# A multi-expert Flamingo block: ScalarE takes the exponential while it evacuates the transposed scores, in both attentions

## The reference, cut to what matters

```python
x = x + tanh(gx[0]) * attention16(layernorm(x), ctx, ctx)   # 16 heads of 8 channels, softmax(q k / sqrt(8)) v
x = x + tanh(gf[0]) * experts_top2(layernorm(x))            # per token: the 2 best of 8 experts
x = x + tanh(gx[1]) * attention1(layernorm(x), ctx, ctx)    # 1 head of 128 channels, causal
x = x + tanh(gf[1]) * experts_choice(layernorm(x))          # per sequence: each of 8 experts picks 17 tokens
```

## Time and profile before

| | |
|---|---|
| time, median of 3 runs | 1260.38 us (1259.9 to 1260.52) |
| profiled execution: span from first to last instruction | 1044.2 us |
| median less that span | 216.2 us |
| TensorE busy | 927.7 us (89%) |
| VectorE busy | 624.5 us (60%) |
| ScalarE busy | 581.2 us (56%) |
| GpSimd busy | 679.4 us (65%) |
| ScalarE, exponentials of layer 0 (L1669) | 32, first 25.7, last 286.1 us |
| ScalarE, exponentials of layer 1 (L1802) | 16, first 618.3, last 708.6 us |

### The profile page before, as it was taken

One profiled execution on the slowest core, in us unless ns is written; L12 is line 12 of the kernel. 1 busy time (PEld: TensorE's weight loads), 2 busy tenths in 40 slices (PEclk: granted clock), 3 DMA queues, 4 the chain that ended last, 5 costly groups with the idle time before them and its releaser, 6 DMA issues.

```text
span 1044.2 us, 25012 instructions
## 1 busy us (share of the span) xinstructions
PE 927.7 (89%) x8892; PEld 777.6 (74%) x8892; DVE 624.5 (60%) x1600; ACT 581.2 (56%) x1274; POOL 679.4 (65%) x905
## 2 busy tenths in 40 slices
PE   5999988788748999999999989887998999999992
PEld 3777776566647989999999977775776767778881
DVE  5899999988964563244625759784735424533320
ACT  2888876687525446544644667554555455444540
POOL 6565556578747777377427777621686758878785
PEclk9999998899868999999999999998999999999997
DMA  9355432122145656676566663123164554574444
GB/s 367 117 177 183 153 123 100 38 67 68 52 157 161 209 176 205 201 213 188 163 193 187 195 236 103 43 71 90 17 114 49 91 68 50 81 105 54 51 54 45
DMA packets 130811, 130.87 MB, mean 125 GB/s; under 512 B 33410, under 2 KB 103426, under 8 KB 129794
## 3 DMA queue, kind: packets, MB, share of 16 engines
q1 hardware_dynamic: 100466, 91.82, 27.8%
q0 software_dynamic: 28928, 29.91, 17.5%
q10 hardware_dynamic: 1296, 7.54, 1.8%
HBM read 54.01 MB, written 49.62 MB: 99 GB/s over the span
## 4 chain that ended last, share of the span: by engine, by line
PE 57%; DVE 13%; ACT 9%; DMA 7%; issue 7%; POOL 6%; ACTq 0%; SPq 0%; POOLq 0%; DVEq 0%
PE psum L844 10%; PE psum L854 10%; PE psum L1022 9%; PE psum L1012 8%; PE psum L656 3%; ACT w_sb L1669 3%; PE psum L976 2%; POOL work L1970 2%; DVE mx L1156 2%; DVE w_sb L1162 2%; ACT work L1676 1%; PE psum L834 1%; DMA out_x<-ln_sb,dest 1%; PE psum L683 1%; DMA odd<-ln_sb,dest 1%
## 5 line engine op out<-in xcount | busy, mean ns | idle before, releaser
L1763 ACT ACTIVATE hid_sb<-psum,work 128x128 f32<-128x128 f32 (+1 forms) x424 | 145.6, 412 | 138.9 <-PE psum L844 136.6
L1970 POOL DMA_INDIRECT work<-yg,place x128 | 122.7, 959 | 73.6 <-issue 48.2
L844 PE MATMUL psum<-work 128*128 128x128 f32 (+1 forms) x848 | 150.1, 320 | 2.6 <-issue 2.3
L854 PE MATMUL psum<-w_sb,hid_sb 128*128 x1192 | 150.2, 275 | 0.0
L854 PEld LDWEIGHTS psum<-w_sb,hid_sb 128*128 128x128 f32 x1192 | 144.8, 192 | 2.1
L1012 PE MATMUL psum<-work,w_sb 128*128 128x272 f32 (+2 forms) x512 | 131.0, 397 | 5.1 <-ACT ctx_sb L1872 3.1
L2044 POOL DMA_INDIRECT out_x<-ln_sb,dest x68 | 106.2, 1562 | 45.0 <-DVE ln_sb L1586 24.8
L844 PEld LDWEIGHTS psum<-work 128*128 128x128 f32 x848 | 124.4, 192 | 11.3 <-issue 4.2
L1872 ACT ACTIVATE ctx_sb<-psum,w_sb 128x272 f32<-128x272 f32 (+2 forms) x256 | 115.8, 488 | 26.3 <-PE psum L1012 22.5
L1022 PE MATMUL psum<-ctx_sb,w_sb 128*128 128x272 f32 (+2 forms) x512 | 128.1, 392 | 0.0
L2044 POOL DMA_INDIRECT odd<-ln_sb,dest x68 | 105.5, 1552 | 32.3 <-issue 16.1
(11 more groups left out here) (241 smaller groups left out, 1762.3 us busy)
## 6 DMA issues: line engine op xcount, KB each, us to landing
work<-w_sb SPq DMA_DIRECT2D x76, 322.0 KB
work<-xg SPq DMA_DIRECT2D x73, 128.0 KB
yg<-yg_sb SPq DMA_DIRECT2D x73, 128.0 KB
xg<-yg_sb SPq DMA_DIRECT2D x24, 384.0 KB, 4.1
ctx_sb<-tok SPq DMA_DIRECT2D x8, 1088.0 KB, 6.4
ctxn<-sums_sb SPq DMA_DIRECT2D x64, 64.0 KB, 2.0
out_x<-x_sb SPq DMA_DIRECT2D x16, 256.0 KB
odd<-yg_sb SPq DMA_DIRECT2D x10, 384.0 KB, 2.9
```

The costliest lines, as they stand in the source:

```text
L844: e.matmul(banks[UP_BANKS[c]][:, 0:cols], w1g(b)[:, c * P:c * P + P], xgT_sb[:, u % 2, at:at + cols], start=True, stop=True).then_inc(s_up, 1)
L854: ins = e.matmul(banks[DOWN_BANKS[b % 2]][:, n * D:n * D + D], hid0[:, b % 2, c, n * P:n * P + P], w2_sb[:, bass.ds(number, 1), c, :].rear ...
L1763: e.activation(hid0[:, b % 2, c, 0:cols], banks[UP_BANKS[c]][:, 0:cols], ACT.Gelu, bias=w1g(b)[:, HID + c:HID + c + 1]).then_inc(s_hg, 1)
L1970: e.indirect_dma_start(dst[:, k, :], None, yg_dram[h], at).then_inc(s_get[i], 16)
```

## The change: what it does

The pass of ScalarE over the row layout is gone in both attentions (L1669 and L1802), with the semaphores that it raised. TensorE transposes the shifted scores themselves, once VectorE has written them. ScalarE's evacuation of the transposed chunks, a copy before, is an activation with the exponential and the scale.

```diff
             def turn_p(p, chunks):
                 i = p % 2
-                w.wait_ge(s_exp, p + 1)
+                w.wait_ge(s_sub, p + 1)
...
             def turn1(g):
-                w.wait_ge(s_e1, g + 1)
+                w.wait_ge(s_sub1, g + 1)
...
-            def exponentials(p):
-                flat = pr[:, p % 2, :, :, :, :].rearrange("p j u h k -> p (j u h k)")
-                w.wait_ge(s_sub, p + 1)
-                e.activation(flat, flat, ACT.Exp, scale=SCALE0).then_inc(s_exp, 1)
-
-            def copy_p(p, chunks):
+            def exponentials(p, chunks):
                 for n in chunks:
                     u, half = n // 2, n % 2
                     w.wait_ge(s_pt, 4 * p + n + 1)
                     w.wait_ge(s_av, p - 1)
-                    e.copy(pT[:, p % 2, u, 4 * half:4 * half + 4, :], banks[B_T[half]]).then_inc(s_pT, 1)
+                    dst = pT[:, p % 2, u, 4 * half:4 * half + 4, :].rearrange("p r q -> p (r q)")
+                    e.activation(dst, banks[B_T[half]], ACT.Exp, scale=SCALE0).then_inc(s_pT, 1)
...
-                if p < NP:
-                    exponentials(p)
...
             def exponentials1(g):
-                flat = p1[:, g % 2, :, :].rearrange("p t k -> p (t k)")
-                w.wait_ge(s_sub1, g + 1)
-                e.activation(flat, flat, ACT.Exp, scale=SCALE1).then_inc(s_e1, 1)
-
-            def copy_p1(g):
                 w.wait_ge(s_pt1, g + 1)
                 w.wait_ge(s_o1, g - 1)
-                e.copy(pT1[:, g % 2, :], banks[3]).then_inc(s_pT1, 1)
+                e.activation(pT1[:, g % 2, :], banks[3], ACT.Exp, scale=SCALE1).then_inc(s_pT1, 1)
...
-                if 0 <= u < NG:
-                    exponentials1(u)
                 if u + 2 < NG:
                     projected1(u + 2)
...
                 if 0 <= u < NG:
-                    copy_p1(u)
+                    exponentials1(u)
```

More of the change, by code:

```diff
@@ L369, in build @@
             "s_ln", "s_lt", "s_lnT", "s_q", "s_qe", "s_k", "s_ke", "s_kx")]
-        s_v, s_vx, s_st0, s_st1, s_sc, s_mx, s_sub, s_exp, s_rden, s_xb, s_uc = [sem(n) for n in (
-            "s_v", "s_vx", "s_st0", "s_st1", "s_sc", "s_mx", "s_sub", "s_exp", "s_rden", "s_xb", "s_uc")]
+        s_v, s_vx, s_st0, s_st1, s_sc, s_mx, s_sub, s_rden, s_xb, s_uc = [sem(n) for n in (
+            "s_v", "s_vx", "s_st0", "s_st1", "s_sc", "s_mx", "s_sub", "s_rden", "s_xb", "s_uc")]
         s_pt, s_pT, s_av, s_sp, s_cn, s_o, s_x1 = [sem(n) for n in ("s_pt", "s_pT", "s_av", "s_sp", "s_cn", "s_o", "s_x1")]
@@ L392, in build @@
             "s_st2", "s_mom1", "s_ln1", "s_lt1", "s_lnT1", "s_g1", "s_ge1", "s_v1", "s_ve1")]
-        s_sc1, s_sub1, s_e1, s_pt1, s_pT1, s_o1, s_x3 = [sem(n) for n in (
-            "s_sc1", "s_sub1", "s_e1", "s_pt1", "s_pT1", "s_o1", "s_x3")]
+        s_sc1, s_sub1, s_pt1, s_pT1, s_o1, s_x3 = [sem(n) for n in (
+            "s_sc1", "s_sub1", "s_pt1", "s_pT1", "s_o1", "s_x3")]
         s_lgT, s_lgt = sem("s_lgT"), sem("s_lgt")
@@ L1730, in scalar_program @@
                 if 0 <= p - 1 < NP:
-                    copy_p(p - 1, (0, 1))
+                    exponentials(p - 1, (0, 1))
                 if g < NG:
@@ L1737, in scalar_program @@
                 if 0 <= p - 1 < NP:
-                    copy_p(p - 1, (2, 3))
+                    exponentials(p - 1, (2, 3))
                 if 0 <= p - 3 < NP:
```

## The result

| | before | after |
|---|---|---|
| time, median (lowest to highest, 4 runs each) | 1260.14 us (1259.89 to 1260.52) | 1247.16 us (1245.11 to 1249.18) |
| profiled execution: time and span | span 1044.2 us, time not given | 1245.11 us, span 1243.3 us |
| ScalarE busy | 581.2 us | 522.9 us |

The ratio is 0.9905, interval 0.9878 to 0.9932: 13.0 us less in the medians (8.6 to 15.4 by the interval), where the prediction said 10.0 with a range of 1247.0 to 1255.0. The 3 us between forecast and measurement are inside the interval. ScalarE's busy time falls by 58.3 us and not by 71.8: rows of one engine overlap a little, and busy time counts an overlap once. Added up row by row, its instructions take 71.7 us less (663.3 to 591.6).

A forecast was written before the change was run, and what follows sets the result against it. Waits on ScalarE's exponential, through its queue, were taken to bound the attentions, with VectorE the bound in layer 1 from 634 to 666 us. 3.5 + 0.7 + 5.3 + 0.6 = 10.1, taken as 10.0: 1250.4 us, range 1247.0 to 1255.0.

The forecast's parts named there:

- Steady part of layer 0: Layer 0 attention, 45 to 150 us: TensorE's waits before L683 of 0.62 and 0.58 fall to 0.26; gain 3.5 us.
- the short pair: Layer 0 steady pairs where TensorE idles only 0.26 us before L683, four of 14; claimed to gain nothing.
- Price of the exponential out of PSUM: Both attentions: each evacuation as exponential costs 0 to 0.10 us more than a copy, taken 0.04, and is covered.
- Tail and start of the experts: End of layer 0 attention gains 0.7 us, layer 0 in all 4.2, passing unchanged through the expert layer.
- Layer 1, first group: Layer 1 attention: L914 no longer waits 1.68 us, the table load hides behind transposes and scores; gain 1.1 us.
- Layer 1, next groups: The 0.27 wait before L914 goes, 0.28 us a group; gain reaches 1.7 us when VectorE takes over at 634.09.
- Catching up: Layer 1 after 666 us: VectorE's idle time lets it follow TensorE, raising the gain from 1.7 to 5.3 us.
- the slow spell goes: Rival, layer 1 near 675 us: TensorE's slow-clock spell, costing 1.6 us, vanishes; 11.6 gained, 1248.8 us; chance 0.12.
- Last group: Layer 1: L914 at 709.25 waits less for the exponential that follows the shift; gain 0.6 us.
- VectorE keeping the gain: Rival, layer 1: idle times after 666 us close, layer 1 gives 1.7 + 0.6, in all 6.5; 1253.9 us; chance 0.20.
- layer 0's wait staying: Rival, layer 0: sums come late for another reason, only layer 1 pays, 5.9 us; 1254.5 us; chance 0.05.
- the clock fall while VectorE leads: Rival, layer 1, 634 to 666 us: TensorE's clock halves, some 4 us more a group, up to 1274; chance 0.04.

The follow-up runs named there:

- e6: Changed kernel with a ScalarE pass nobody waits for put back at the old queue place in 30 of 32 layer 0 pairs; 1246.34 us, ratio to before 0.9895.
- e4: Kernel before with only the layer 1 part of the change; 1252.83 us, ratio 0.9953.
- e8: Changed kernel with all gathers and puts of layer 0 replaced by plain DMAs of rows in order; 1019.15 us, ratio to before 0.8103.
- e11: Changed kernel, layer 0 puts and gathers waiting for those of two tiles before, not four; chip 4, without stalls; 1036.14 us, ratio to before 0.9926.
- e1: Kernel before, unchanged, run and profiled again; 1259.69 us, span 1260.8 us.
- e2: Changed kernel, unchanged, run again; 1248.85 us, ratio to before 0.9902.
- e3: Kernel before with only the layer 0 part of the change; 1255.62 us, ratio 0.9949.
- e7: Changed kernel with only the layer 0 gathers replaced by plain DMAs of rows in order; 1120.12 us, ratio to before 0.8898.
- e9: Changed kernel with a bound on the row numbers of layer 0's 128 gathers and 128 puts; 1249.0 us, ratio to before 0.9957.
- e12: Kernel before with all layer 0 puts and gathers as plain DMAs of rows in order; 1031.62 us, ratio to before 0.8192.

## Why the prediction was right, and where it was off

**The mechanism** held: in layer 0 the steady gain is the time that the pass stood in the queue (e6), and in layer 1 TensorE no longer waits for it before the transposes (e4, e8). The size was 13.0 us by the first runs, 11.9 and 12.5 later, against 10.0; on the chip without stalls e11 gave 8.1. So the forecast lies inside what was measured, and the sizes of its terms have to be judged one by one.

**Steady part of layer 0**, predicted 3.5 us. Measured 97.7 less 93.2 = 4.5 over 13 pairs, the same within 0.1 us in every pair of traces. What was mis-sized is the floor of the wait, by the reading of the short pair: "0.26 is what the copy itself costs and no edit to the exponential removes it". The trace of before has ScalarE's rows of both kinds of pair (the second copy is in the earlier trace rows):

```profile
98.98 1.94 ACT L1669 ACTIVATE w_sb<-w_sb 128x2048 f32<-128x2048 f32 x1
100.80 0.60 ACT L1683 COPY sums_sb<-psum 128x512 f32<-128x512 f32 x1
106.43 1.93 ACT L1669 ACTIVATE w_sb<-w_sb 128x2048 f32<-128x2048 f32 x1
```

The copy at 108.23 starts 0.13 us before the exponential ends (108.36), just as the one at 100.80 starts 0.12 before its own (100.92). Both kinds of pair were bound by the queue. All 14 waits of the changed kernel are 0.18: over the 13 pairs, with three of the short ones, 7 x 0.44 + 3 x 0.40 + 3 x 0.08 = 4.5.

**Price of the exponential out of PSUM**: taken 0.04, measured 0.006 us in layer 0. It was covered there: L673 does not wait for it in the rows above.

**Tail and start of the experts**, predicted 4.2 us in all. Without stalls the first L834 comes 7.0 us earlier in one pair of traces (318.3 to 311.3) and 2.5 in the other (305.6 to 303.1). With stalls it comes at 338.7 and 340.4 with the old layer 0 (e4, e1) and at 332.2 to 337.9 with the new one (after, e2, e3, e7, e9), 4.2 between the means. The spread lies behind the steady part: from the 15th to the 21st pair single executions of either kernel take 59.6 to 62.3 us. The tail's 0.7 could not be told from that.

**Layer 1, first group**, predicted 1.1: the first L924 comes 11.7 us after the last L854 in before (e1, e12) and 10.6 in the changed kernel (after, e8). In the trace of 1044.2 us it is 12.9 and in e11 13.9, so this distance holds other waits too; from the L892 that stands ahead of it (616.23 in before, 804.10 in after) it is 4.33 or 4.34 us in all three traces of before and 3.29 or 3.30 in after, e8 and e11: 1.0 us. The evacuation, load and exponential follow as in the sum. The drain of some 1.4 us that the rule of the Trainium skill ("ScalarE: Activation LUTs", section "What ACT_TABLE_LOAD costs") would add is not in these rows either: 806.74 less 805.45 is 1.29. The prediction also says that a load does not wait for its operand. The rows that it names could not show this, since VectorE's shift had ended before the load; another place in the trace of before does:

```profile
314.36 1.28 ACT L1763 ACT_TABLE_LOAD   x1
321.11 0.47 ACT L1763 ACTIVATE hid_sb<-psum,work 128x256 f32<-128x256 f32 x1 [5.46 <-PE psum L844]
```

**Layer 1, next groups**, predicted 0.28 each and the gain then held at 1.7. Measured, in e12 and e8, 5.12 us a group become 4.69, and from the first output matmul to that of the sixth group 2.2 us are gained, of the seventh 1.5. So the price of a group was too low, 0.28 for 0.43. VectorE did take over, but at the seventh group and not at the fourth (634.09 in the trace of before): there L914 waits 1.42 us for its shift. The missing 0.15 are in how the idle time is counted, up to the modelled end of L892. TensorE's timeline in e12, then in e8:

```profile
618.84 1.05 PE L892 MATMUL psum<-w_sb,ctx_sb 128*128 128x128 f32 x8
620.17 0.66 PE L914 MATMUL psum<-ident,work 128*128 128x128 f32 x4 [0.28 <-ACT work L1802]
```

```profile
614.16 1.05 PE L892 MATMUL psum<-w_sb,ctx_sb 128*128 128x128 f32 x8
615.05 0.60 PE L914 MATMUL psum<-ident,work 128*128 128x128 f32 x4
```

From start to start it is 1.33 us with the wait and 0.89 without: where nothing holds L914, it starts 0.16 us before the end that the trace gives for L892. In the next group of e8 the distance is 0.95.

**Catching up**: by the eleventh group the gain behind the first is 5.9 us (61.6 to 55.7 in this pair), where the forecast had 4.2. VectorE's waits there shrink as forecast: 1.58, 0.62 and 2.55 us in e12, 1.09 in e8. Of the rest 1.6 were the rival's: **the slow spell goes**. The tenth output matmul took 1.93 us in both traces of before without stalls and takes 1.06 in e7, e8 and e11; from the L906 ahead of it to the L885 behind it there are 3.86 us in e12 and 2.22 in e8. The clock granted in e12 in 636 to 670 us is 0.95, in e8 1.00. I gave this 0.12 beside the forecast and not on top of it; what came is both, where there are no stalls. With stalls the tenth output matmul takes 1.06 us in before too (e1), so the 13.0 us of the result owe nothing to this rival at this place; slow spells stand at other groups there, in both kernels.

**Last group**, predicted 0.6 gained. Its output matmul comes 5.4 us behind that of the group before in e12, and 7.4 in e8, 6.3 in e7 and 6.1 in e11: 0.7 to 2 us lost. From VectorE's shift to L914 the forecast holds (1.41 us in e12, 0.75 in e8). But the shift comes late, and L914 waits 4.54 us for it in e8: ahead of it VectorE waits for a DMA that brings a token list for the last experts, longer in e8 than in e12. The forecast had no term for the wait on this DMA. VectorE in e12, then in e8:

```profile
692.28 0.36 DVE L1531 TENSOR_SCALAR ctx_sb<-ctx_sb,rowcol_sb 128x272 f32<-128x272 f32 x1 [1.33 <-DMA ctx_sb<-tok]
```

```profile
683.53 0.36 DVE L1531 TENSOR_SCALAR ctx_sb<-ctx_sb,rowcol_sb 128x272 f32<-128x272 f32 x1 [2.94 <-DMA ctx_sb<-tok]
```

**Sum without stalls**, e12 against e8 and e7: 4.5 + 1.1 + 5.2 to 6.3 = 10.8 to 11.9 us, beside a measured 12.5. The two spans do not show this sum: they differ by 7.2 us (1029.5 and 1022.3), since of the 4.4 us gained in the steady pairs 1.9 are lost again before the experts start, and 1.1 more in the rest. The profiled execution of e8 was its slowest (1024.15 us for a median of 1019.15). Where the median executions differ outside the steady pairs and layer 1 is not known.

**The 216.2 us** by which the median lies above the span, "which I take as fixed", were wrong in what they are and, by luck, right in effect. They are stalls inside the span that the trace of before did not have, and they neither grew nor shrank with the change beyond their spread.

**Rivals.** VectorE keeping the gain and layer 0's wait staying did not happen. Nor did the clock fall while VectorE leads, in e8, where there are no stalls: it is 1.00 from 625 to 666 us.

## What to carry to other kernels

An engine that is no bound can still hold another up by what stands in its queue. To find the floor of such a wait, look at whether the waited-for instruction starts behind its operand or at the end of its neighbour in the queue, in the shortest wait too. Compare the span of the page with the times of the runs before any sum: here they differed by 216 us, and the page was of another condition than the one that was timed. And where single runs spread by 10 us, a term of 3 us is settled by the length of its stage in the trace, not by the time.

## What the runs showed of the hardware

- The same kernel took 1044.2 us on one chip and 1253 to 1261 on two others. The difference lies where GpSimd issues many indirect DMAs of layer 0 one behind the other at 1.25 us each: TensorE then starts matmuls 0.7 or 2.1 us apart and further, without a wait in the trace, and ScalarE and VectorE stand nearly idle (0.42 and 1.42 us busy in 20 for VectorE and ScalarE, 700 to 720 us of after). Plain DMAs of as many bytes, of rows in order, remove it: e8 lies 228 us under after. Some 17 of these are not stalls, since e8 also lies 17 us under e11, which has none.
- Layer 1's 136 indirect DMAs take 1.55 us each and follow each other at 1.85 us in rows of at most 22; no stall shows there (330.2 to 333.0 us for the rest in every condition). A bound on the row number is not what makes the difference (e9). Open are the pace, the adding, the scattered rows, and why one chip is free of it. The traces with stalls also hold fewer semaphore events, 14,229 in e1 against 19,114, so that recording itself is part of the cause cannot be excluded.
- A table load of ScalarE takes 1.28 us and does not wait for the operand of the activation behind it: 314.36 us in before, with the operand ready only at 321.11. In ten of the twelve loads of after the next activation starts 1.29 us after the load's start.
- An exponential with a scale that reads 128x512 f32 from PSUM takes 595 ns and a copy 589; with a bias vector an activation of that size takes 689.
